# Attention stage of a graph network: ScalarE copies the gathers' block numbers between its two groups of rows

## The chip, the cores and the metric

One core of a Trainium2 chip. The metric is the device time of one execution in microseconds (us); the median of three executions is given. The engines are TensorE (PE; its weight loads are PEld), VectorE (DVE), ScalarE (ACT), GpSimd (POOL) and SyncE (SP), which only issues transfers here.

## What is computed

Four graph layers run over 6250 nodes with 128 features and 106250 edges. The change lies in the fourth, an attention with five anchors:

```
combined = concatenate([x[src], x[dst]], axis=1)
b   = softmax(leaky_relu(combined @ edge_w.T + edge_b, 0.01), axis=1)
ep  = b @ edge_anchor
agg = zeros_like(xp).at[src].add(ep).at[dst].add(ep)
return xp + 0.5 * agg
```

The products of `x` with the two halves of `edge_w` are five numbers for each node. They are made once (P for the source side, Q for the destination side). For each edge the kernel then looks P up by its source and Q by its destination, adds them, makes the softmax, and adds the five weights to the source node and to the destination node.

## The kernel before, in words

The edges lie in 832 tiles of 128. One iteration of the attention loop takes 16 tiles (four groups of four), so there are 52 iterations; the loops' bodies hold two iterations, `u` = 0 and 1, because most buffers are doubled. The engines work it as one pipeline, each with its own hand-written order, and meet at semaphores:

- POOL (lines 854 to 862) fetches P for 12 of the 16 tiles: it waits for `idx16` (the block numbers of that iteration have been copied) and for `logits_done` (the buffer `p_rows[u]` was read two iterations before), then it issues 12 indirect DMAs, line 767. They read `p_table` and count on the semaphore `gathered[u]`.
- ACT (lines 1252 to 1262), in iteration `it`: `rows_ahead(it + 1, 1 - u, g)` for g = 0 and 1, then the exponentials `y5` (line 1258), then `stage_16(it + 2, u)` (line 1173), which copies the 16 block numbers of iteration it + 2 into `stage16[u]` for POOL, then `copy_sources` (line 1196), then `rows_ahead` for g = 2 and 3. `rows_ahead` makes the one-hot rows of the destinations (lines 939 to 945) and, for g = 0 and 1, those of the sources (lines 1183 and 1191). Ahead of line 1183 it waits on `scattered` until TensorE's by_source products of the same group of the iteration before have read the buffer.
- PE (lines 1708 to 1735), in iteration `it`: waits for `logits_done`; looks Q up for the first group of it + 1 (line 1661); turns the source rows (1686); looks P up for four tiles (1694); then four times: look-up of another group (1661) and `by_source` (1667, fp32); at the end 32 small `by_destination` products (1672).
- DVE (lines 2712 to 2782), in iteration `it`: waits for `gathered[u]` and for `q_looked` (the four look-ups of line 1661); sums the logits (2755); adds the fetched rows (2757, which counts `logits_done`); leaky relu, maximum, subtraction (2761 to 2763, `soft_in`); columns (2729); after the exponentials the softmax's sum, reciprocal and products (2768 to 2770), the parts, the matrices for by_source (2749), and `take_sources` (2703 to 2707).
- SP loads the destinations of a group, 256 KB, each time that ACT has read the former ones at line 940.

The lines that set the order around the change are these.

```
act.wait_ge(soft_in, it + 2)
nc.scalar.activation(y5, z5, ACT.Exp).then_inc(soft_exp, 1)
stage_16(it + 2, u)
copy_sources(it + 1)
```

```
pool.wait_ge(idx16, it + 1)
pool.wait_ge(logits_done, it + 1)
for t in range(LOOKED, L16):
    gather(p_rows[u][:, t, :], p_table, stage16[u][:, t:t + 1], gathered[u])
```

`idx16` is counted twice ahead of the loop and `logits_done` starts at 2, so POOL's iteration it + 2 needs ACT's copy and DVE's line 2757 of iteration it.

Of the kernel before, what the change touches and what calls it, by code (L numbers as in the profile page):

```python
# [28 lines left out]
LOOKED = 4  # L29
# [4 lines left out]
ITERS = GROUPS // 4  # L34
# [39 lines left out]
def gnn_stack(nc, x, src, dst, edge_type, Wl1, bl1, Wr1, gamma0, beta0, Wl2, bl2, Wr2,  # L74
# [3 lines left out]
    with ctx:  # L78
# [3 lines left out]
        def sem(name):  # L82
            return ctx.enter_context(nc.semaphore(name))
# [176 lines left out]
        L16 = 4 * GT  # L260
# [122 lines left out]
        gathered = [sem(f"gathered{g}") for g in range(4)]  # L383
# [29 lines left out]
        logits_done = sem("logits_done")  # L413
# [453 lines left out]
        def _(act):  # L867
# [65 lines left out]
            def one_hot_rows(it, g, to, used, used_at, meanwhile=None):  # L933

                k = it * 4 + g
                act.wait_ge(dst_in[g % 2], 16 * (it * 2 + g // 2 + 1))

                act.wait_ge(used, used_at)
                nc.scalar.activation(to[0], dst_b[g % 2][:, :], ACT.Abs, bias=neg_row[0][:, bass.ds(k, 1)])
                nc.scalar.activation(to[1], dst_b[g % 2][:, :], ACT.Abs, bias=neg_row[1][:, bass.ds(k, 1)]).then_inc(oht_abs, 1)  # L940
                if meanwhile:
                    meanwhile()
                act.wait_ge(oht_abs, k + 3)
                nc.scalar.activation(to[0], to[0], ACT.Relu, bias=1.0, scale=-1.0)
                nc.scalar.activation(to[1], to[1], ACT.Relu, bias=1.0, scale=-1.0).then_inc(oht_ready, 1)
# [221 lines left out]
            relu_hidden()  # L1167
            sqrt(sd[:, :], var[:, :], 2 * DENSE + 5 + CHUNKS_IN_PASS)

            def stage_16(it, u):  # L1170

                act.wait_ge(logits_done, it + 1)
                nc.scalar.activation(stage16[u][:, :], p_row_i[:, bass.ds(it * L16, L16)], ACT.Copy).then_inc(idx16, 1)  # L1173

            def rows_ahead(it, u, g):

                lo = lo_l3[u][:, g * GT:(g + 1) * GT, :]

                def source_distances():

                    act.wait_ge(scattered, 4 if isinstance(it, int) else it * 4 + g - 3)
                    for j in range(GT):
                        last = nc.scalar.activation(lo[:, j, :], iota[:, 0:P], ACT.Abs,
                                                    bias=neg_lo[:, bass.ds(it * L16 + g * GT + j, 1)])
                    last.then_inc(lo_abs, 1)

                one_hot_rows(it, g, [oht_l3[:, g, h, :] for h in range(2)], q_looked, it * 4 + g + 1,
                             source_distances if g < 2 else None)
                if g < 2:
                    act.wait_ge(lo_abs, it * 2 + g + 1)  # L1190
                    nc.scalar.activation(lo, lo, ACT.Relu, bias=1.0, scale=-1.0).then_inc(lo_ready, 1)

            def copy_sources(it):

                act.wait_ge(src_turned, it + 1)
                nc.scalar.activation(src_rows, bank[6][:, 0:LOOKED * P], ACT.Copy).then_inc(src_copied, 1)
# [48 lines left out]
            copy_projected(steps_of(PROJ) - 1)  # L1245
            act.wait_ge(zeros_done, 1)
            stage_16(0, 0)
            stage_16(1, 1)
            copy_sources(0)
            act.wait_ge(soft_in, 1)  # L1250
            nc.scalar.activation(n5[0], n5[0], ACT.Exp).then_inc(soft_exp, 1)
            with act.Fori(0, ITERS // 2) as i2:
                for u in range(2):
                    it = i2 * 2 + u
                    for g in range(2):
                        rows_ahead(it + 1, 1 - u, g)
                    act.wait_ge(soft_in, it + 2)
                    nc.scalar.activation(y5, z5, ACT.Exp).then_inc(soft_exp, 1)
                    stage_16(it + 2, u)
                    copy_sources(it + 1)  # L1260
                    for g in range(2, 4):
                        rows_ahead(it + 1, 1 - u, g)
# [1571 lines left out]
```

## Time and profile before

| | us |
|---|---|
| median of 3 executions | 5300.39 (5296.77 to 5312.35) |
| the profiled execution | 5294.73 |
| its span, first to last instruction | 5292.9 |
| PE busy | 3378.9 (64%) |
| DVE busy | 2400.0 (45%) |
| POOL busy | 2265.7 (43%) |
| ACT busy | 1369.7 (26%) |

The attention loop lies in the last quarter of the span, from about 4100 to 5270 us. A row of the timeline is one or several instructions of one line in order of time; the bracket behind it gives the idle time of the engine and what ended it. "remote" stands where the profile could not tell what ended it, and "issue" where the engine waited for nothing that the profile shows.

### The profile page before, as it was taken

How to read it: one execution, taken by the hardware profiler on the slowest of the kernel's cores; microseconds unless marked ns; L12 is line 12 of the kernel's file. 1: busy time of each engine (PE TensorE's matmuls, PEld its weight loads, DVE VectorE, ACT ScalarE, POOL GpSimd, SP SyncE). 2: the span in 40 equal slices, each digit the busy share in tenths (PEclk: the TensorE clock that was granted, in tenths of full speed). 3: DMA queues.
4: the chain of work that ended last, by engine and by line, in shares of the span. 5: the costliest groups of instructions: out<-in, count | busy, mean ns of one | idle time of the engine just before them, and what ended most of it. 6: DMA issues, size and time to landing. Idle time of an engine off the chain costs nothing.

```text
span 5292.9 us, 65458 instructions
## 1 busy us (share of the span) xinstructions
PE 3378.9 (64%) x18669; PEld 2194.1 (41%) x18670; DVE 2400.0 (45%) x6266; ACT 1369.7 (26%) x3030; POOL 2265.7 (43%) x2364
## 2 busy tenths in 40 slices
PE   2699996998734334333333376676696577777776
PEld 2254453444422222222223343333344455555555
DVE  5866666334612222222222222222247566666666
ACT  2655551000400000000000000000002566666665
POOL 3000001000066666666656666666621555555552
PEclk7799998999856666666655577777797666777767
DMA  2211113221712222222221122323230222222222
GB/s 76 59 75 76 50 74 125 84 87 73 202 47 64 68 70 64 69 68 65 69 62 45 46 82 80 90 81 84 79 93 23 45 50 51 50 50 50 50 51 60
DMA packets 265797, 368.93 MB, mean 70 GB/s; under 512 B 64035, under 2 KB 194634, under 8 KB 260666
## 3 DMA queue, kind: packets, MB, share of 16 engines
q1 hardware_dynamic: 187830, 248.24, 14.7%
q0 software_dynamic: 74464, 114.31, 10.2%
q10 hardware_dynamic: 3364, 4.69, 0.3%
q8 instruction: 68, 1.11, 0.1%
q14 instruction: 71, 0.58, 0.0%
HBM read 261.10 MB, written 105.93 MB: 69 GB/s over the span
## 4 chain that ended last, share of the span: by engine, by line
PE 33%; issue 19%; another core or an unknown queue 16%; DVE 14%; POOL 12%; DVEq 3%; DMA 2%; ACT 1%; ACTq 1%; POOLq 0%; SPq 0%
PE psum L1478 14%; POOL GS L767 12%; PE psum L1391 4%; PE psum L1410 4%; PE psum L1348 3%; DVE GS L2074 2%; DMA GS<-xw_table,stage 1%; DVE O L2749 1%; DVEq L2074 1%; PE psum L1543 1%; PE psum L1369 1%; DVE HT L2729 1%; PE psum L1594 1%; PE psum L1595 1%
## 5 line engine op out<-in xcount | busy, mean ns | idle before, releaser
L767 POOL DMA_INDIRECT GS<-xw_table,stage x1664 | 1576.4, 947 | 1440.7 <-issue 1073.0
L1410 PE MATMUL psum<-GS 128*128 128x96 f32 x3328 | 607.8, 343 | 601.5 <-DMA GS<-xw_table,stage 462.3
L1478 PE MATMUL psum<-HA,HT 128*128 128x512 fp8e4 (+1 forms) x3822 | 852.2, 370 | 38.8 <-DVE HT L2258 38.8
L767 POOL DMA_INDIRECT HA<-p_table,stage x624 | 600.5, 962 | 579.4 <-ACT stage L1173 354.2
L1410 PEld LDWEIGHTS psum<-GS 128*128 128x128 f32 x3328 | 566.5, 254 | 650.6 <-issue 638.6
L2088 DVE TENSOR_TENSOR HA<-HA,psum 128x96 f32 x208 | 52.9, 255 | 1584.9 <-remote 1143.2
L2074 DVE TENSOR_SCALAR GS<-iota,HT,wt 128x96 f32<-128x96 f32 x1680 | 453.1, 354 | 213.5 <-issue 212.2
L1478 PEld LDWEIGHTS psum<-HA,HT 128*128 128x128 bf16 x3822 | 360.0, 99 | 370.9 <-DVE HT L2258 39.4
L1369 PE MATMUL psum<-Wcat,codes 128*128 128x512 f32 x196 | 177.8, 1062 | 459.9 <-DVE codes L2567 395.5
L1127 ACT ACTIVATE HA<-psum 128x392 fp8e4<-128x392 f32 x784 | 349.7, 495 | 261.8 <-PE psum L1348 238.7
L876 ACT ACTIVATE stage<-edge_cols 128x16 int32<-128x16 int32 (+1 forms) x104 | 22.1, 215 | 1315.0 <-remote 853.0
L1391 PE MATMUL psum<-Wcat,HT 128*128 128x512 fp8e4 (+1 forms) x1080 | 303.2, 430 | 66.9 <-issue 51.1
L1667 PE MATMUL psum<-O,HA 128*128 128x245 f32 x832 | 252.1, 461 | 40.0 <-issue 20.8
L1369 PEld LDWEIGHTS psum<-Wcat,codes 128*128 128x128 f32 x196 | 56.7, 319 | 519.0 <-issue 519.0
L1667 PE MATMUL psum<-O 128*128 128x245 f32 x832 | 246.3, 451 | 38.3 <-issue 20.3
L1348 PE MATMUL psum<-edge_cols 128*128 128x196 bf16 x1568 | 239.1, 260 | 48.3 <-ACT HA L1127 28.9
L882 ACT ACTIVATE HT<-psum 128x512 f32<-128x512 f32 x49 | 29.3, 597 | 846.7 <-PE psum L1370 608.0
L2749 DVE TENSOR_TENSOR O<-HA,psum 128x980 f32<-128x980 f32 x208 | 242.8, 1167 | 0.0
L1667 PEld LDWEIGHTS psum<-O,HA 128*128 128x128 f32 x832 | 191.0, 239 | 76.7 <-issue 41.3
L1667 PEld LDWEIGHTS psum<-O 128*128 128x128 f32 x832 | 185.7, 233 | 71.3 <-DVE O L2749 25.7
L1391 PEld LDWEIGHTS psum<-Wcat,HT 128*128 128x128 bf16 x1080 | 118.2, 113 | 221.9 <-issue 153.9
L1348 PEld LDWEIGHTS psum<-edge_cols 128*128 128x128 bf16 x1568 | 117.5, 99 | 214.5 <-ACT HA L1127 92.0
(414 smaller groups left out, 4687.6 us busy)
## 6 DMA issues: line engine op xcount, KB each, us to landing
HT<-dst_rows SPq DMA_DIRECT2D x212, 256.0 KB
xw_table<-HT SPq DMA_DIRECT2D x100, 512.0 KB, 3.2
adj<-HA SPq DMA_DIRECT2D x13, 3136.0 KB, 9.1
GS<-xw_table,stage POOLq DMA_INDIRECT x1664
Wcat<-adj SPq DMA_DIRECT2D x45, 512.0 KB
HA<-adj SPq DMA_DIRECT2D x13, 1600.0 KB
HA<-adj SPq DMA_DIRECT2D x13, 1536.0 KB
HA<-adj SPq DMA_DIRECT2D x20, 512.0 KB
```

The source lines that it names most:

```text
L767: nc.gpsimd.indirect_dma_start(out=to, out_offset=None, in_=table, in_offset=bass.IndirectOffsetOnAxis(ap=idx, axis=0)).then_inc(done, 16)
L1127: nc.scalar.activation(placed_at[s][:, :, i * 8:i * 8 + 8].rearrange("p b (w d) -> p b w d", d=NODES_IN_TILE), bank[6 + i % 2][:, 0:2 * KE ...
L1348: last = nc.tensor.matmul(bank[6 + h][:, j % 2 * KEYS:(j % 2 + 1) * KEYS], by_lo[k % 4][:, j, :], by_key[k % 4][:, j, :], start=True, stop ...
L1369: nc.tensor.matmul(bank[2 + c][:, :], own, Wcat[1][:, c * 4 * P:(c + 1) * 4 * P], start=True, stop=True)
L1391: last = nc.tensor.matmul(bank[2 + n % 4][:, 0:w], Hs4[:, CHUNK * c + i, t, :], chunk_tile[place_of(n)][:, i * GW:i * GW + w], start=(i == ...
L1410: last = nc.tensor.matmul(bank[h][:, 0:WINDOW], G3[g][:, j, :], S_pair[h][:, t, :], start=(t == 0), stop=(t == 2 * GT - 1))
L1478: last = nc.tensor.matmul(bank[s][:, 0:w], Hs4[:, b, t, :], adj_tile[s][:, b * GW:b * GW + w], start=(b == 0 and t == 0), stop=(b == SRCS ...
L1543: nc.tensor.matmul(bank[s][:, 0:w], Hs4[:, FINAL + i, t, :], chunk_tile[place_of(n)][:, i * GW:i * GW + w], start=(i == 0 and t == 0), sto ...
L1594: nc.tensor.matmul(bank[2 + 2 * s][:, :], tT[s][:, 0:P], Wcat[0][:, 0:4 * P], start=True, stop=True)
L1667: return nc.tensor.matmul(bank[2][:, 0:245], lo_l3[u][:, t, :], M_l3[:, t, :], start=False, stop=False, skip_group_check=True)
L2074: last = V.tensor_scalar(S_pair[s][:, j, :], iota[:, 0:WINDOW], dl_pair[:, bass.ds(k * 2 * GT + j, 1)], wt[:, bass.ds(k * 2 * GT + j, 1)], ...
L2749: V.tensor_tensor(M_l3[:, at, :].rearrange("p j (d a) -> p j d a", a=A5), hi_l3[:, at, :].unsqueeze(3).broadcast_to([P, GT, 49, A5]), b5[: ...
```

## The change

`stage_16(it + 2, u)` moves ahead of the exponentials, between `rows_ahead` of group 0 and `rows_ahead` of group 1. In place of its wait for `logits_done` it waits inside the loop for `gathered[u]`: that the gathers of iteration it, which read the same `stage16[u]`, have landed. The two copies ahead of the loop wait for nothing now. Nothing else is changed: POOL still waits for `idx16` and `logits_done`, and the order of DVE, PE and SP stays.

```diff
-            def stage_16(it, u):
-
-                act.wait_ge(logits_done, it + 1)
+            def stage_16(it, u, rounds=None):
+
+                if rounds is not None:
+                    act.wait_ge(gathered[u], 64 * 2 * ITERS + 16 * (L16 - LOOKED) * rounds)
                 nc.scalar.activation(stage16[u][:, :], p_row_i[:, bass.ds(it * L16, L16)], ACT.Copy).then_inc(idx16, 1)
...
                     it = i2 * 2 + u
-                    for g in range(2):
-                        rows_ahead(it + 1, 1 - u, g)
+                    rows_ahead(it + 1, 1 - u, 0)
+                    stage_16(it + 2, u, i2 + 1)
+                    rows_ahead(it + 1, 1 - u, 1)
                     act.wait_ge(soft_in, it + 2)
                     nc.scalar.activation(y5, z5, ACT.Exp).then_inc(soft_exp, 1)
-                    stage_16(it + 2, u)
                     copy_sources(it + 1)
```

## Rows read from the trace of the kernel before

**Rows 1.** The page: span; costliest groups (busy, mean ns | idle before, releaser).

```profile
span 5292.9 us, 65458 instructions
...
L767 POOL DMA_INDIRECT HA<-p_table,stage x624 | 600.5, 962 | 579.4 <-ACT stage L1173 354.2
```

**Rows 2.** Waits, 4200 to 5200 us: us in total, times, longest us.

```profile
DVE HA L2755 <- remote: 350.9, 46, 7.7
POOL HA L767 <- ACT stage L1173: 325.8, 46, 7.2
...
PE psum L1672 <- issue: 153.1, 142, 2.0
```

**Rows 3.** Timeline of one iteration, DVE, ACT and POOL: start, us, instruction.

```profile
4598.18 0.41 DVE L2755 TENSOR_REDUCE HA<-psum 128x80 f32<-128x240 f32 x1 [7.60 <-remote]
...
4601.97 0.21 ACT L1173 ACTIVATE stage<-edge_cols 128x16 int32 x1
...
4602.98 1.07 POOL L767 DMA_INDIRECT HA<-p_table,stage  x1 [7.06 <-ACT stage L1173]
...
4612.44 0.61 ACT L1191 ACTIVATE O<-O 128x512 f32<-128x512 f32 x1
...
4616.93 0.94 POOL L767 DMA_INDIRECT HA<-p_table,stage  x1 [0.30 <-issue]
...
4620.12 0.41 DVE L2755 TENSOR_REDUCE HA<-psum 128x80 f32<-128x240 f32 x1 [7.60 <-remote]
4620.13 1.28 ACT L1183 ACTIVATE O<-iota,edge_cols 128x128 f32<-128x128 f32 x4 [5.85 <-remote]
...
4621.23 0.23 DVE L2757 TENSOR_TENSOR HA<-HA 128x80 f32<-128x80 f32 x1
...
4624.94 1.06 POOL L767 DMA_INDIRECT HA<-p_table,stage  x1 [7.06 <-ACT stage L1173]
```

**Rows 4.** Timeline of PE in the same iteration.

```profile
4606.43 3.63 PE L1667 MATMUL psum<-O 128*128 128x245 f32 x8 [1.04 <-DVE O L2749]
...
4610.12 1.93 PE L1667 MATMUL psum<-O 128*128 128x245 f32 x8
4611.89 0.35 PE L1661 MATMUL psum<-HA 128*128 x8
4612.09 3.56 PE L1667 MATMUL psum<-O 128*128 128x245 f32 x16
4615.78 0.17 PE L1672 MATMUL psum<-HA,HT 128*128 128x15 bf16 x1
...
4619.99 1.16 PE L1672 MATMUL psum<-HA,HT 128*128 128x15 bf16 x28 [0.54 <-issue]
```

**Rows 5.** Timeline of DVE, the last two iterations.

```profile
5235.36 0.41 DVE L2755 TENSOR_REDUCE HA<-psum 128x80 f32<-128x240 f32 x1 [7.67 <-remote]
...
5250.01 0.41 DVE L2755 TENSOR_REDUCE HA<-psum 128x80 f32<-128x240 f32 x1 [0.30 <-PE psum L1661]
```

**Rows 6.** Windows: stretch, us, busy (x instructions) of PE, PEld, DVE, ACT, POOL; PEclk.

```profile
4200.00:5200.00 1000.00, 718.31 (x5104) 561.99 (x5104) 647.84 (x1556) 630.11 (x1322) 522.59 (x544) 0.70 0.25 50
...
4602.98:4615.70 12.72, 11.64 (x60) 9.13 (x59) 9.44 (x18) 9.82 (x19) 9.67 (x11) 0.72 0.34 69
4615.70:4619.95 4.25, 0.68 (x4) 0.45 (x4) 0.00 (x0) 0.00 (x0) 1.87 (x2) 1.00 0.36 53
...
4619.95:4622.28 2.33, 1.91 (x38) 1.78 (x38) 2.16 (x11) 2.15 (x6) 0.00 (x0) 0.60 0.00 0
4622.28:4624.93 2.65, 1.42 (x14) 0.86 (x13) 2.62 (x7) 1.88 (x6) 0.00 (x0) 0.50 0.00 0
```

**Rows 7.** Windows of other runs of gathers: start of the attention loop, second hop.

```profile
4163.16:4172.20 9.04, 7.95 (x69) 6.24 (x68) 8.94 (x18) 6.68 (x11) 7.01 (x7) 1.00 0.32 66
4172.20:4180.30 8.10, 3.08 (x8) 1.72 (x8) 0.68 (x1) 4.06 (x9) 4.71 (x5) 0.78 0.20 38
...
3113.54:3127.50 13.96, 13.63 (x67) 8.17 (x65) 5.37 (x20) 0.00 (x0) 10.61 (x12) 0.82 0.32 86
3127.50:3135.90 8.40, 3.97 (x10) 1.13 (x11) 0.00 (x0) 0.00 (x0) 4.53 (x5) 0.78 0.38 109
```

## The prediction

> **What bounds the kernel now.** I read the page first, for the gathers of `p_table`: 624 of them, 962 ns each, and 354.2 us of POOL's idle time end with ACT's copy of the block numbers, line 1173 [rows 1]. That is the wait that the edit goes at. Then the list of waits over 1000 us of the attention loop, for who waits longest: DVE stands 350.9 us at the first operation of its iteration, line 2755, 46 times, 7.6 us each [rows 2]. Then the timeline of one iteration, for the order of events. It repeats from iteration to iteration: line 2755 starts at 4598.18 and at 4620.12, so the period is 21.94 us; there are 48 such periods between the start of the loop and its last iteration.
>
> Counted from line 2755 at 4598.18, POOL's first gather starts at 4.80, right after the copy at 3.79; the twelfth ends at 4617.87, that is 19.69; and the next line 2755 starts 2.25 after that [rows 3]. So the period reads as 4.80 until the gathers start, 14.89 of gathers and 2.25 behind them. The last iteration has no gathers beside it, and its period is 14.65 (5235.36 to 5250.01) [rows 5]. The gathers cost 7.3 us an iteration.
>
> How they cost it decides this case. DVE does not wait there for the gathers in flight: they are those of the iteration after, as ACT has copied their block numbers only in this iteration. Left is `q_looked`. The look-up that it needs last was in PE's array at 4611.89 [rows 4], and DVE went on at 4620.12. ACT's line 1183 was released in the same moment, 4620.13 [rows 3]; it waits for the by_source products that ended at 4612.05 [rows 4]. And PE itself slowed down: after 4615.78 its small products came one in 1.4 or 0.7 us, until 4619.99, when 28 went through in 1.16 us [rows 4]. So three engines are held until about 2.1 us after POOL's last gather. What holds them is PE's side: its products are done but not reported.
>
> The windows show how PE comes to be held. I count matmuls and weight loads together and call them PE instructions. The loop has (5104 + 5104)/45.5 = 224 of them an iteration [rows 6]. From the first gather on, PE did 119 at full pace in 12.72 us, then 8 in 4.25 us [rows 6]. At the start of the loop, with another spacing, it was 137 in 9.04 us, then 16 in 8.10; in the second hop 132 in 13.96 us, then 21 in 8.40 [rows 7]. Three stretches of gathers with the same picture: PE gets through 119 to 137 instructions, then crawls at about 2 a microsecond until the gathers are over. I read this as an allowance in instructions: during the 17.0 us of a hold (14.89 + 2.1) it is 119 + 8 = 127 here, 153 at the start of the loop, and about 132 + 3.1 x 2.5 = 140 in the hop. The other 100 or so of an iteration must be done in the gap between a release and the next first gather. That gap is 4.98 us now and holds 76 + 27 = 103 of them [rows 6].
>
> The Trainium skill, "NOTIFIC — the notification-queue block", section 7.1, says that the block which writes out the instruction records holds its producers back when its internal queues are full rather than lose a record, and that its stall counter would show an engine throttled that way. That is a rule that speaks against this change, since it, too, would make the hold a matter of PE's instruction count; no run here shows that this block is the cause, and by it the sum would be that of the forecast below.
>
> **The change, part by part.**
>
> The copy itself: 0.21 us on ACT [rows 3], moved, not added. It now stands behind line 1191 of group 0, which starts at 4612.44 and ends at 4613.05, so at about 14.9 of the iteration before. It delays group 1 of the rows by 0.2 us at most; behind it on ACT stand lines 939 and 940 of group 1 and, through line 940, one of SP's four loads. ACT idles 5.85 us right behind these [rows 3], so this costs nothing as long as ACT is held there. The look-up copy behind the exponentials comes 0.1 us earlier, which is worth nothing.
>
> The new wait, for the gathers of iteration it: they ended before the line 2755 of iteration it - 1, some 15 us before ACT comes to it. Cost 0 now. If they were late, the six ACT operations of group 1, the exponentials and so DVE's softmax would stand behind it; I see nothing that would make them so late.
>
> What it brings: POOL no longer waits for the copy, only for line 2757, which ends at 4621.46. From the copy's end (4602.18) to the first gather it took 0.80 [rows 3]; the same from 4621.46 gives 4622.26, 2.14 us into the iteration in place of 4.80. So each run of gathers starts up to 2.66 us earlier. I take 2.65.
>
> What is late next: the gap. If the gathers start 2.65 us earlier, the gap is 4.98 - 2.65 = 2.33 us. In its first 2.33 us PE did 76 instructions; the other 27, those of 4622.28 to 4624.93, move under the gathers [rows 6]. Until the small products begin, PE now needs 119 + 27 = 146 in the hold; it has 127 to 153, and the row nearest to this loop's steady state says 127. With 127, 19 are left over, that is 9 or 10 by_source matmuls. They run after the release at 0.24 to 0.45 us each (1.93 and 3.63 us for 8) [rows 4], 2.2 to 4.5 us, and the 64 cheap instructions of line 1672 (1.2 us) come behind them instead of in the gap. So the next hold starts with some 60 more to do, PE does not reach the look-ups before it, and DVE has to wait for them after the release. The lag does not heal: the gathers start 2.14 us after line 2755 however late PE is.
>
> **The sum.** In the state that this runs into, a period is: hold 17.0, then PE's work from where it was held to the last look-up, then 2.1 to the next gather. PE instructions: 224 less 140 in the hold (middle of 127 and 153) less some 16 in the last 2.1 us (by_source at 0.24 to 0.45 us for two) leaves 68. That is two groups of by_source, two groups of look-ups (64 instructions) and a little: 2 x 1.93 + 2 x 0.35 = 4.6 us at the high clock, 2 x 3.63 + 0.7 = 8.0 at the low one. I take 5.7, near the high one, since PE idles more and the granted clock was 1.00 in the crawl [rows 6]. Period 17.0 + 5.7 + 2.1 = 24.8, 2.85 more than now; times 48 is 137 us. Against the profiled execution, 5294.7, that is 5431.7; I say 5430. The median of the three runs is 5.7 us above the profiled one, less than my uncertainty, and I leave it out. With 153 in the hold 55 remain, about 4.1 us, period 23.2, +1.3, 5356; with 127 and the low clock 9 us or more, 28.1, 5590. This case's own range is 5355 to 5590.
>
> **Rivals.**
>
> 1. The hold ends with the gathers whatever PE has to do. Then the period is 2.14 + 14.89 + 2.25 = 19.3; 2.65 x 48 = 127 us less, 5168. For it: DVE's wait of 7.6 us is 7.7 at its longest in 46 iterations [rows 2], so the release does follow the gathers closely as long as PE's look-ups are through, and 153, as at the start of the loop, would be enough for 146 [rows 7]. Against: in the steady state the crawl begins at 119 [rows 6].
>
> 2. The gathers start early only in part. Group 0's by_source is reported at about PE instruction 82 of a hold instead of 55; if that report is held, ACT's copy comes 3 us after the release, POOL starts at 3.8, the period is 20.9 in such iterations: 5294.7 - 48 x 1.0 = 5245. Alternating with case 1 it is 5206.
>
> 3. No gain: the gap settles near 4.9 us again by one delay or another, or the new wait keeps the copy as late as it was: 5295.
>
> The deciding point between rival 1 and the forecast is whether PE can do 146 instructions in a hold.
>
> **Chances.** Forecast, slower: 0.57. Rival 1: 0.15. Rival 2: 0.18. Rival 3: 0.10. The prediction is 5430. The range of 8 in 10 leaves out rival 1 (0.15) and the top of the slow case (0.05): 5200 to 5520. About 0.3% is what a measurement of this kernel can tell from no change; faster by more than that 0.33, within it 0.10, slower 0.57.
>
> **What would show it.** In the profile after: the list of waits no longer has POOL waiting for ACT's copy in either case. First step: first gather 2.1 to 2.2 us after line 2755. Second step: in a hold PE crawls while by_source, line 1667, is not yet finished (before, only line 1672 crawled), and by_source matmuls follow line 2755. Third step: line 2755 comes 4 us or more after the release instead of 0.1, ended by PE's look-up, line 1661, and the period is 23 us or more. If line 2755 keeps coming 2.25 us after the last gather with a period of 19.3, the reading of the hold as an allowance is wrong. If POOL waits for ACT's copy again, it is rival 2.

## The result, and the profile after

The changed kernel took 5508.91 us in the median of four executions (5471.09 to 5531.02), the kernel before beside it 5303.64. The ratio is 1.0378, with a 95% interval of 1.0319 to 1.0438: slower, by 205 us. The profiled execution took 5528.67 us with a span of 5526.9. That it is slower was forecast, and that PE's work would lie behind the gathers and make DVE wait; what keeps PE back is another thing than the one forecast, as the traces below show. The forecast of 5430 is 79 us short of the median, which lies 11 us inside the upper end of the range, 5520. A later run showed something that the prediction had no row for: on another chip of the same kind the same change costs nothing (change_again, below).

All but some 10 us of the loss arises between the first and the last iteration of the attention loop, so the loop is to be read. Its iterations again start at the reduction of the logits, which is now line 2756. These are three of its rows in the timeline of DVE: the first of a steady iteration, one in the middle, and the last iteration.

```profile
4166.26 0.40 DVE L2756 TENSOR_REDUCE HA<-psum 128x80 f32<-128x240 f32 x1
...
4716.49 0.41 DVE L2756 TENSOR_REDUCE HA<-psum 128x80 f32<-128x240 f32 x1 [2.36 <-PE psum L1662]
...
5468.23 0.40 DVE L2756 TENSOR_REDUCE HA<-psum 128x80 f32<-128x240 f32 x1
```

From the first to the last row are 49 periods: 1301.97 / 49 = 26.57 us on average, where it was 21.94 for the one of [rows 3]. Most are 27.4 long, and eight of the 49 lie between 21.9 and 22.7. Note what ended the idle time: PE's look-up of the logits, line 1662, 2.36 us. In [rows 3] this wait was 7.60 us and "remote".

The list of waits over the same 1000 us as [rows 2] names what is new (who waited for whom, us in total, times, longest):

```profile
ACT HT L1197 <- remote: 471.9, 38, 14.8
...
PE psum L1695 <- ACT HT L1197: 315.5, 29, 13.3
POOL HA L767 <- ACT stage L1174: 281.3, 23, 12.8
DVE HT L2730 <- remote: 246.8, 106, 4.2
POOL HA L767 <- DVE HA L2758: 127.8, 14, 12.7
```

In what follows a report is the semaphore count by which PE tells another engine that a product is done; the hold is the time from the first gather of an iteration until the reports are through again, and its end, some 2 us behind the last gather, is the release.

ACT stands 12.4 us each time in front of its copy of the turned source rows, line 1197, and PE stands behind it in front of the look-up of P, line 1695. DVE's long wait at the reduction is gone; instead it waits at line 2730 (the columns), which needs PE's by_destination products. The timeline of PE, in the iteration that starts at 4716.49, shows the order (start, us, instruction, idle before and what ended it):

```profile
4716.31 3.56 PE L1668 MATMUL psum<-O 128*128 128x245 f32 x16
4719.71 1.20 PE L1673 MATMUL psum<-HA,HT 128*128 128x15 bf16 x32
4720.98 0.46 PE L1662 MATMUL psum<-HA 128*128 x8
4721.30 0.64 PE L1687 MATMUL psum<-ident,O 128*128 128x128 f32 x3
4722.26 0.31 PE L1687 MATMUL psum<-ident,O 128*128 128x128 f32 x1 [0.32 <-issue]
4722.98 0.23 PE L1662 MATMUL psum<-HA 128*128 x3 [0.40 <-issue]
4724.40 0.25 PE L1662 MATMUL psum<-HA 128*128 x3 [1.20 <-issue]
4725.13 0.17 PE L1662 MATMUL psum<-HA 128*128 x1 [0.47 <-issue]
4736.54 2.68 PE L1695 MATMUL psum<-HT 128*128 128x250 bf16 x12 [10.52 <-ACT HT L1197]
4739.02 2.75 PE L1668 MATMUL psum<-O,HA 128*128 128x245 f32 x8
...
4718.77:4722.60 3.83, 3.41 (x50) 2.62 (x48) 2.14 (x5) 3.30 (x9) 2.92 (x4) 1.00 0.35 71
4718.77:4726.10 7.33, 4.25 (x58) 3.12 (x56) 2.83 (x6) 3.30 (x9) 5.65 (x6) 0.84 0.23 39
```

The last two rows are windows from the first gather on, with the columns of [rows 6]: PE instructions, as the prediction counts them, are 50 + 48 by the time that the rows are turned, and 58 + 56 when PE stops. And ACT and POOL in the same iteration, then DVE's columns:

```profile
4717.76 0.20 ACT L1174 ACTIVATE stage<-edge_cols 128x16 int32 x1
...
4721.82 0.25 ACT L1260 ACTIVATE HA<-HA 128x80 f32<-128x80 f32 x1
4735.89 0.60 ACT L1197 ACTIVATE HT<-psum 128x512 bf16<-128x512 f32 x1 [13.82 <-remote]
...
4718.77 0.94 POOL L767 DMA_INDIRECT HA<-p_table,stage  x1 [12.10 <-ACT stage L1174]
...
4733.32 0.94 POOL L767 DMA_INDIRECT HA<-p_table,stage  x1 [0.30 <-issue]
...
4723.14 0.69 DVE L2730 TENSOR_TENSOR HT<-rows,wt 128x1024 bf16<-128x1024 bf16 x1 [2.20 <-remote]
4727.39 0.69 DVE L2730 TENSOR_TENSOR HT<-rows,wt 128x1024 bf16<-128x1024 bf16 x1 [3.55 <-remote]
...
4730.26 0.69 DVE L2730 TENSOR_TENSOR HT<-rows,wt 128x1024 bf16<-128x1024 bf16 x1 [2.04 <-remote]
```

PE had turned the rows, line 1687, by 4722.57. ACT was free from 4722.07 and got the report at 4735.89, 1.63 us after the last gather had ended. So for 13.3 us the work was done and not reported. The by_destination products ahead of it (line 1673) were all done by 4720.91, and DVE, which needs one group of them for each of its columns, went on with the second at 4723.14, the third at 4727.39 and the fourth at 4730.26, all while gathers still ran. So a late report needn't wait for the release: they come in PE's order, some 3 to 6 us apart here, and the one for the turned rows is far back in the row. In the kernel before, ACT's same copy waited for PE only three times in 53, and that 3.2 us in all. The period reads 2.28 until the first gather, 17.12 from there to the release at 4735.89, and 8.05 of PE's work behind it (copy, look-up of P, two groups of by_source, two of logits): 27.45. In the eight short iterations the same report came 8.7 to 10.8 us behind the first gather, as in the one that starts at 4611.04, with its first gather at 4613.64:

```profile
4624.42 0.60 ACT L1197 ACTIVATE HT<-psum 128x512 bf16<-128x512 f32 x1 [7.48 <-remote]
```

### The profile page after: what moved, and what is told of

It reads as the page before. It is cut to its first block, busy times and chain, and to the rows that moved or that the text cites. A ratio compares the mean times of both kernels' runs of the same rounds, so it can differ in the third digit from the quotient of the medians.

```text
span 5526.9 us, 65405 instructions
## 1 busy us (share of the span) xinstructions
PE 3275.2 (59%) x18669; PEld 2137.6 (39%) x18670; DVE 2421.6 (44%) x6266; ACT 1359.5 (25%) x3030; POOL 2288.8 (41%) x2364
## 3 DMA queue, kind: packets, MB, share of 16 engines
q1 hardware_dynamic: 187830, 248.24, 14.2%
## 4 chain that ended last, share of the span: by engine, by line
PE 35%; another core or an unknown queue 24%; issue 15%; POOL 10%; ACT 7%; DVE 6%; DVEq 2%; ACTq 1%; DMA 1%; POOLq 0%; SPq 0%
PE psum L1479 14%; POOL GS L767 10%; PE psum L1392 3%; PE psum L1349 3%; PE psum L1411 3%; PE psum L1668 3%; PE psum L1695 2%; PE psum L1544 1%; DMA GS<-xw_table,stage 1%; DVE GS L2075 1%; ACT HA L940 1%; DVEq L2075 1%; ACT HA L939 1%; ACT O L1184 1%
## 5 line engine op out<-in xcount | busy, mean ns | idle before, releaser
L767 POOL DMA_INDIRECT HA<-p_table,stage x624 | 622.7, 998 | 772.6 <-ACT stage L1174 353.7
L1695 PE MATMUL psum<-HT 128*128 128x250 bf16 x636 | 139.7, 407 | 492.9 <-ACT HT L1197 426.3
L2730 DVE TENSOR_TENSOR HT<-rows,wt 128x1024 bf16<-128x1024 bf16 x208 | 143.6, 692 | 347.5 <-remote 328.6
L1695 PEld LDWEIGHTS psum<-HT 128*128 128x128 bf16 x636 | 85.5, 142 | 537.3 <-ACT HT L1197 438.6
L1668 PE MATMUL psum<-O,HA 128*128 128x245 f32 x832 | 218.1, 414 | 13.4 <-issue 12.3
L1668 PE MATMUL psum<-O 128*128 128x245 f32 x832 | 219.9, 416 | 7.4 <-issue 5.3
```

The source lines that it names most:

```text
L767: nc.gpsimd.indirect_dma_start(out=to, out_offset=None, in_=table, in_offset=bass.IndirectOffsetOnAxis(ap=idx, axis=0)).then_inc(done, 16)
L1668: return nc.tensor.matmul(bank[2][:, 0:245], lo_l3[u][:, t, :], M_l3[:, t, :], start=False, stop=False, skip_group_check=True)
L1695: last = nc.tensor.matmul(looked_p[j], src_rows[:, j * P:(j + 1) * P], Pp_part[t], start=(t == 0), stop=(t == PARTS - 1))
L2730: V.tensor_tensor(S_in_fours[:, g, :, :], row_code, dl_b[:, bass.ds(it * L16 + g * GT, GT)].unsqueeze(1).broadcast_to([P, 2 * P, GT]), ALU ...
```

## The experiments

The count theory is the prediction's: PE gets through a limited number of instructions in a hold, and the change asks for more. Beside it stand three others. Order: ACT's new order or its new wait costs the time. Chain: the report of the turned rows falls under the gathers. Report: the general form of it, built on the first four runs: only the first few dozen PE instructions behind the first gather report at once, the others mostly at the release. The kernels ran on several chips. On some the kernel before takes 5303 to 5335 us, on others 4582 to 4589; which it was stands with each run and turned out to matter.

**The start alone.** To the changed kernel one wait of POOL is added:

```diff
                     pool.wait_ge(logits_done, it + 1)
+                    pool.wait_ge(soft_exp, it + 1)
```

> The changed kernel with one wait more: POOL starts its gathers only after the exponentials of the iteration (some 4.9 us after line 2756, as in the kernel before, where it was 4.80). ACT's new order and its new wait stay. Two theories say that the early start alone costs the time: the count theory of the prediction (PE gets through 119 to 153 instructions under the gathers and needs 146) and the chain theory (the report that PE has turned the source rows falls under the gathers, so ACT's copy of them and PE's look-up of P stand until the release). Both expect period 21.9 to 22.1, 5290 to 5320 us, and ACT's line 1197 some 3.9 us after line 2756. The order theory (ACT's copy between its two groups, or the wait on the gathers, costs the time) expects 5450 to 5550, as in the changed kernel.

Measured: 5303.51 us, ratio 0.9998 (0.9989 to 1.0008), before at 5302.83. ACT's order and its wait on the gathers cost nothing when the gathers start late: the order theory falls. The loss comes with the early start of the gathers. The next kernel has the same with soft_in, one step earlier.

> The changed kernel with one wait more: POOL starts after DVE's subtraction of the maxima (line 2764), just ahead of the exponentials, some 4.4 us after line 2756 in place of 2.1 (changed) and 4.8 (before). The chain theory expects that PE's turn is reported by 3.9 us, ahead of the first gather, so that ACT's line 1197 stays at 3.9 us and 0.4 us an iteration is won: period 21.5, 5275 to 5290 us. The count theory expects 107 instructions wanted more in the hold per 0.4 us of 10 a microsecond, that is 123 against 127 to 153: no loss, the same 5275 to 5290, or a first sign of lag, up to 5350. The order theory expects 5450 to 5550.

Measured: 5298.18 us, ratio 0.9994 (0.9984 to 1.0004). No lag, but no gain clear of the noise either, so the expected 13 to 28 us are missing. POOL's rows, in the iteration whose line 2758 starts at 4686.64, show where they are:

```profile
4691.10 1.42 POOL L767 DMA_INDIRECT HA<-p_table,stage  x1 [6.56 <-DVE HA L2766]
4692.82 1.04 POOL L767 DMA_INDIRECT HA<-p_table,stage  x1 [0.30 <-issue]
...
4705.40 0.94 POOL L767 DMA_INDIRECT HA<-p_table,stage  x1 [0.31 <-issue]
```

The first gather takes 1.42 us here and 1.07 in [rows 3]. The last one ends 19.70 us into the iteration, with a start at 4.46, and in [rows 3] at 19.69, with a start at 4.80. The earlier start is lost within the first gather, which takes 0.35 us more; what stretches it was not tried.

**The wait taken from PE.** The look-up of P uses the copy of the iteration before:

```diff
-                pe.wait_ge(src_copied, it + 1)
...
-                        last = nc.tensor.matmul(looked_p[j], src_rows[:, j * P:(j + 1) * P], Pp_part[t],
+                        last = nc.tensor.matmul(looked_p[j], src_rows2[u][:, j * P:(j + 1) * P], Pp_part[t],
```

> The changed kernel, where PE's look-up of P for the first four tiles doesn't wait for ACT's copy of this iteration but uses the copy of the iteration before, in a second buffer; all four look-ups go to one PSUM bank. The number and order of PE's instructions stay at 224 an iteration, and the gathers start early. Left out: the P terms of the first four tiles are not those of their edges. The count theory expects it slow still, since the number of instructions is the same: period 23 or more, 5360 to 5530 us. The chain theory expects that PE no longer stands 10.5 us in front of line 1695: PE goes on to its allowance, and after the release 2.7 us of look-ups and at least one group of by_source (1.9 to 3.6 us) are no longer to be done; period 19.5 to 23, 5180 to 5340 us.

Measured: 5487.34 us, ratio 1.0364 (1.0335 to 1.0392), before at 5302.83. The count theory's range holds it; that of the chain theory doesn't. But the run separates them less than I meant it to. Its waits over 1000 us of the loop are:

```profile
ACT GS L1198 <- remote: 239.1, 20, 14.6
DVE HT L2732 <- remote: 202.2, 95, 5.5
ACT HT L1198 <- remote: 196.2, 17, 15.0
...
4645.31:4662.46 17.15, 9.71 (x75) 6.11 (x74) 8.53 (x19) 3.31 (x10) 12.15 (x12) 0.64 0.15 18
```

I had freed PE, not ACT: its copy still stands 435.3 us in 37 times, with the rows of groups 2 and 3 queued behind it, which PE needs for the logits. That DVE waits for by_destination, too, says that more reports than one are late.

The last row, a window of one of its holds from the first gather to ACT's copy, says more than the time does. PE didn't stop: it did 75 + 74 = 149 instructions, more than the 146 that the prediction wanted. Even so line 2758 came 6.2 us behind the release, at 4668.64, as PE stood 1.87 us at line 1663 for the rows that ACT makes behind its copy, and had a group of by_source and the last logits behind that. So in this kernel PE's count was met and the time was lost all the same, by the report that ACT got late.

**64 instructions fewer.** The changed kernel without the by_destination products:

```diff
-                        for j in range(GT):
-                            last = by_destination(g * GT + j, at[g], S_in_fours[:, g, :, j])
-                        last.then_inc(scattered_d, 1)
+                        pe.sem_inc(scattered_d, 1)
```

> The changed kernel without the 32 by_destination matmuls and their 32 weight loads; PE counts their semaphore itself. Left out: the sums by destination. 160 instructions an iteration are left of 224, 82 of the 146 that had to be done under the gathers. The count theory expects the hold to cost nothing more: period 19.3, 5160 to 5200 us. The chain theory expects that the turned rows are still reported only after the gathers have begun (turn about 4.5 us after line 2756 in the lagging state, gathers from 2.1), so the lagging state stays in most iterations: period 25 to 26.5, 5400 to 5480 us.

Measured: 5282.90 us, ratio 0.9960 (0.9946 to 0.9974), before at 5302.83. Both theories miss. The period is 21.6 us (line 2754 at 4600.02 and 4621.66), and the reason is in three groups of rows: PE's windows from the first gather at 4602.12 (the columns are those of [rows 6]), PE's look-up of P, and ACT and DVE where they take PE's results.

```profile
4602.13:4604.40 2.27, 2.27 (x20) 1.79 (x18) 2.24 (x7) 2.27 (x7) 1.97 (x2) 0.89 0.22 75
4602.13:4607.10 4.97, 4.17 (x39) 3.17 (x37) 4.87 (x14) 4.91 (x12) 4.05 (x4) 0.95 0.19 55
...
4605.58 1.47 PE L1695 MATMUL psum<-HT 128*128 128x250 bf16 x12 [0.75 <-issue]
...
4604.93 0.60 ACT L1197 ACTIVATE HT<-psum 128x512 bf16<-128x512 f32 x1
...
4619.30 0.67 DVE L2702 TENSOR_TENSOR HT<-psum,HT 128x490 f32<-128x490 f32 x1 [7.30 <-remote]
```

The turned rows were done by the 38th PE instruction of the hold (20 + 18), and ACT took them at once. The look-up of P was done by the 76th, at 4607.05, and DVE got it 12.25 us later, at the release. Behind that lie DVE's lines 2702 to 2706, 2.4 us, and they are on the path. With the gathers from 2.10: 2.10 + 15.1 + 2.1 + 2.4 = 21.7. So within one hold an early report passes and a later one doesn't. From this I formed the report theory, though the rows of the changed kernel, with reports that trickle in while gathers run, don't fit its "only".

**One report moved, in the kernel before.** It is the direct test; the number of PE instructions stays, and the gathers start as before:

```diff
-                        if g == 0:
+                        if g == 1:
                             look_up_sources(it + 1)
```

> The kernel before with one thing moved: PE's look-up of P stands behind by_source of group 0 and the logits of group 2 (place g == 1) instead of ahead of them, so it ends about 50 to 58 instructions after the first gather instead of 18; the gathers start at 4.8 us as before. The report theory expects its report to be held until the release in most iterations; DVE then does lines 2702 to 2707 (2.4 us) behind the release: period 24.2, 5380 to 5415 us. The count theory expects no change, since PE does the same number of instructions: 5295 to 5310 us.

The chip was one where the kernel before takes 4582.15 us: 4656.10, ratio 1.0162 (1.0145 to 1.0179). Here DVE's wait at line 2703 is ended by PE's matmul itself each time, 117.4 us in 53, so the report isn't late: it is the look-up that is. A repeat came to such a chip, too:

> The kernel before with PE's look-up of P moved behind by_source of group 0, as in late_p_look_up (on a chip without the hold it came to 1.0162 of before, as DVE waited up to 2.7 us for the look-up). On a chip with the hold the report theory expects the look-up to be the 50th to 58th instruction after the first gather, reported only at the release, 2.4 us of DVE's work behind the release: period 24.2, 5380 to 5415 us. The count theory expects 5295 to 5310 us. On a chip without it: 1.016 again.

4658.88 against 4589.08, ratio 1.0151 (1.0134 to 1.0168). The third came to one where the kernel before takes 5335.05:

> The kernel before with PE's look-up of P moved behind by_source of group 0, once more (on a chip without the hold it was 1.016 and 1.015 of before). On a chip with the hold (before near 5300) the report theory expects: the look-up is the 50th to 58th PE instruction after the first gather in place of the 18th, PE's instructions stay at 224, and the look-up's report comes at the release; DVE waits some 7 us at line 2703 and does its 2.4 us of lines 2703 to 2707 behind the release; period 24.2, 5380 to 5415 us. The count theory expects 5295 to 5310 us, as PE has no more to do than before. On a chip without the hold: 1.015 again.

Measured: 5448.47 us, ratio 1.0215 (1.0198 to 1.0233), that is 113 us or 2.3 an iteration. The count theory expected no change. PE, its windows and DVE of one iteration:

```profile
4708.45 2.19 PE L1694 MATMUL psum<-HT 128*128 128x250 bf16 x12
...
4701.10:4710.70 9.60, 5.96 (x31) 4.69 (x31) 7.33 (x15) 8.40 (x17) 7.25 (x8) 0.54 0.37 85
...
4718.46 0.67 DVE L2703 TENSOR_TENSOR HT<-psum,HT 128x490 f32<-128x490 f32 x1 [9.97 <-remote]
...
4720.83 0.40 DVE L2755 TENSOR_REDUCE HA<-psum 128x80 f32<-128x240 f32 x1
...
4745.18 0.40 DVE L2755 TENSOR_REDUCE HA<-psum 128x80 f32<-128x240 f32 x1
```

The look-up was done at 4710.64, as about the 62nd instruction (31 + 31) behind the first gather at 4701.31, and DVE, which had stood there since 4708.49, got it at 4718.46. Reported at once, it would have held DVE 2.2 us, far ahead of the release. Then its three lines, then line 2755: the period is 24.35, for 24.2 expected. The expected 5380 to 5415 us were reckoned from a kernel before of 5303, as 77 to 112 us more; it was 113 more. The same edit costs 70 to 74 us on the chips without a hold, too, where the iteration is some 7 us shorter and DVE comes to the look-up before it is done; that is another wait.

**The chain moved ahead, with an early start.** The turn stands ahead of by_destination, ACT's copy ahead of its group 1, the look-up of P first in the iteration:

```diff
+                    copy_sources(it + 1)
                     rows_ahead(it + 1, 1 - u, 1)
...
+                    look_up_sources(it + 1)
                     pe.wait_ge(logits_done, it + 2)
...
+                    pe.wait_ge(p_taken, it + 2)
+                    turn_sources(it + 2, u)
                     pe.wait_ge(parts5, it + 2)
```

> The changed kernel (gathers from 2.1 us) with the chain of the turned rows moved: PE turns the source rows of the next iteration right behind the last by_source group, ahead of the by_destination products; ACT copies them ahead of group 1 of the rows; PE looks up P first thing in the iteration. Number of PE instructions unchanged, 224. The report theory, formed on the runs so far, says: of the PE instructions that run after the first gather only about the first 35 to 45 report their end at once, the later ones mostly at the release 2.1 us after the last gather; in the changed kernel the turn (about the 94th) is held. It expects the look-up of P to be among the first 35 here, no wait of 10 us at line 1197, DVE released with the gathers: period 19.3 to 21.0, 5170 to 5260 us. The count theory of the prediction (146 instructions wanted under the gathers, 119 to 153 to be had) expects no cure: 5360 to 5530 us.

> The same moved chain, with POOL held back until DVE's line 2765 just ahead of the exponentials, first gather at 4.45 us. Report theory and count theory both expect the period to be set by the gathers: 21.7 to 21.9, 5285 to 5305 us. A time over 5320 would say that the moved chain itself costs something (the turn ahead of by_destination, or ACT's copy ahead of group 1), to be taken off the result of turn_ahead.

Both came to the chip without a hold: 4677.67 us, ratio 1.0208 (1.0191 to 1.0225), and 4677.32, ratio 1.0209 (1.0192 to 1.0226). The start of the gathers makes no difference there; the moved chain itself costs 2%, some 95 us. Their numbers say nothing on the hold, so the first was run again:

> The kernel of turn_ahead (gathers from 2.1 us, PE's turn ahead of by_destination, ACT's copy ahead of group 1, PE's look-up of P first in the iteration), once more, since its first run came to a chip whose traces show no hold (there 1.021 of before, DVE waiting for its turned rows at 17.1 us a period). If the chip holds PE's reports (before near 5300), the report theory expects the look-up of P among the first 35 PE instructions after the first gather, so that DVE is released with the gathers: period 19.3 to 21.5, 5170 to 5280 us. The count theory expects 5360 to 5530 us. The turn itself stands about 120 instructions into the hold, so its report comes at the release in either case; where ACT's copy, now ahead of its group 1, is what PE then waits for, the period could be 22 to 24. If the chip doesn't hold them: 1.021 again.

With the kernel before at 5303.38 it took 5615.75 us, ratio 1.0593 (1.0575 to 1.0611). Both theories expected less, the report theory by 335 us or more. Why, PE's windows from the first gather at 4706.16 and DVE's rows tell:

```profile
4706.15:4707.90 1.75, 1.75 (x29) 1.63 (x28) 1.72 (x7) 0.44 (x1) 1.44 (x2) 1.00 0.04 1
4706.15:4708.50 2.35, 2.31 (x41) 2.10 (x39) 2.31 (x7) 1.04 (x2) 1.97 (x2) 1.00 0.04 2
4706.15:4710.20 4.05, 3.79 (x54) 3.28 (x52) 2.31 (x7) 2.74 (x7) 3.13 (x4) 1.00 0.04 2
...
4711.98 0.69 DVE L2732 TENSOR_TENSOR HT<-rows,wt 128x1024 bf16<-128x1024 bf16 x1 [3.48 <-remote]
4723.30 0.69 DVE L2732 TENSOR_TENSOR HT<-rows,wt 128x1024 bf16<-128x1024 bf16 x1 [10.62 <-remote]
```

I had misplaced the look-up of P: with the 64 instructions of by_destination ahead of it and PE still behind at the first gather, it is not among the first 35 but done by the 106th (54 + 52). And by_destination itself, done by the 80th, is now under the gathers: DVE's columns wait 10.62 us for it, in the middle of the softmax, so by_block and with it PE's by_source start only behind the release. The mechanism is the same; the move put one more report where it is held. What part of the 312 us is the cost of the moved chain itself was not taken apart.

**Half the gathers.**

> The changed kernel with six gathers an iteration in place of twelve. Left out: the P rows of six of the sixteen tiles are not fetched. Gathers run from 2.1 to 9.6 us after line 2756, release at 11.7. The report theory expects the turned rows still to be reported only at the release, and line 2756 some 8 us after that: period 19 to 20, 5150 to 5200 us. The count theory expects PE never to reach its allowance, as 119 instructions take it longer than the gathers do: period 14.7 to 16, 4940 to 5010 us.

It came to the chip without a hold: 4529.33 us, ratio 0.9886 (0.9869 to 0.9902), before at 4582.15. An iteration takes 14.2 us there (line 2756 at 4111.7 and 4125.9), so six gathers are hidden altogether. How the hold scales with the number of gathers is left open.

**The change itself, again.**

> The changed kernel, unchanged, beside a run of the kernel before on the same chip. On the chip of the last four runs the kernel before took 4582 us in place of 5303, and in their traces PE was never held under gathers. Report theory, if the chip is one that holds PE's reports (before near 5300): 5470 to 5530 us, as first measured. If it is one that doesn't (before near 4580): the early start costs nothing and there is no hold to get rid of; the copy no longer has to be waited for, period 14.9 to 15.3 against some 15.1: 4560 to 4590 us, within 0.5% of before. A rival, that the early gathers collide with something else (SP's loads, DVE) whatever the reports do, expects 1 to 4% slower on either chip.

Measured beside a kernel before of 4589.08 us: 4588.45, ratio 0.9998 (0.9988 to 1.0008). Two of its rows of DVE, and ACT's line 1197 over the whole run (duration, first and last start):

```profile
4204.53 0.41 DVE L2756 TENSOR_REDUCE HA<-psum 128x80 f32<-128x240 f32 x1 [1.39 <-DMA HA<-p_table,stage]
...
4219.51 0.41 DVE L2756 TENSOR_REDUCE HA<-psum 128x80 f32<-128x240 f32 x1 [0.53 <-DMA HA<-p_table,stage]
...
L1197 ACT ACTIVATE HT<-psum x53: 570/577/598, 3738.8 to 4545.9; 128x512 bf16<-128x512 f32 x53
its engine sat idle before it (us, times) until:
  PE psum L1687: 9.1, 16
```

The period is 14.98 us here and 15.3 on average over the loop, POOL's gathers run back to back, and DVE waits a little for their data: 12 x (0.94 + 0.30) = 14.9 is the bound. ACT's copy waits for PE 9.1 us in all, where it was 617.5 us in 49 times in the first trace of the same kernel. So on this chip gathers run through the whole iteration, beside SP's loads and DVE's work, and cost little beyond their own time; the rival with the collision expected 1 to 4% and doesn't hold there. No trace of the kernel before was kept from such a chip, so how early its gathers start is not known.

## Why the prediction was right, and where it was off

**First gather at 2.1 to 2.2: right.** It is 2.10 to 2.84 us, 2.28 in the iteration shown. In this iteration the copy, not line 2758, was last: ACT's group 0 was late, as PE was. POOL still has waits for ACT's copy in its list, which the prediction took as a sign of rival 2; here they come from PE's lag, and the period is longer, not shorter.

**A hold until about 2 us behind the last gather: right.** 17.12 us from first gather to release against 17.0.

**Why PE falls behind: right that it does, wrong in what decides.** The step that failed is "PE now needs 146 in the hold; it has 127 to 153". PE never came to use that allowance: it stopped after 114 (58 + 56) because the look-up of P needs a report from PE to ACT and one back, and the first came at the release. In early_old_sources, where PE didn't have to wait for it, PE got to 149, so 127 wasn't the limit, and the kernel was slow all the same (5487.34). The prediction read the crawl of PE as the hold's only price for PE and counted instructions. [Rows 3] and [rows 4] already had the other half: three engines held by products that were done and not reported. Which reports still pass was the thing to ask. Taken together the traces say that those done by the 38th instruction (early_no_dst) passed, and that those done by the 62nd (late_p_third) and the 76th (early_no_dst) came only with the release; in the kernel before the look-up of P was done by the 22nd, and its early place was what kept 21.94. The change moved the turn to about the 98th. And the changed kernel's own rows show that a late report can come before the release: by_destination 4723.14, 4727.39 and 4730.26, the turned rows in eight iterations 8.7 to 10.8 us behind the first gather. They fit a queue of reports that empties slowly while gathers run better than a fixed line; that is a reading, no run tests it.

Of the second sign, by_source behind line 2756 came (4716.31, 3.56 us), but PE's slow pace fell on lines 1662 and 1687, not on by_source, and began after 98 instructions, where the prediction had 119 to 137.

**Line 2756 late, ended by PE's line 1662: right; its size was the mis-sized term.** The forecast had 5.7 us of PE's work behind the release, for 68 instructions. It was 8.05 us, for 88: two groups of by_source and two of logits, as forecast (4.7 us of the 5.7), but the copy and the look-up of P, 0.65 + 2.68 us, came on top. The period was then 27.45 in place of 24.8 in most iterations. In eight the report came earlier, as at 4624.42, which is 10.8 us behind the first gather in place of 17.1, and the period was 22.34; that pulled the mean to 26.57. The prediction knew nothing of these, and they are why the median lies within its range: 27.45 throughout would be some 43 us more, by these rows above 5520. That part is luck. Against the sum: 26.57 less 24.8 is 1.77, times 49 is 87 us; the start of the loop adds 8.8; 5431.7 + 87 + 9 = 5527, and the profiled execution took 5528.67.

**Rivals.** The hold ended with the gathers for DVE and ACT but left PE with work, so rival 1 (19.3) didn't come about on the chips that hold. Rival 2 had a held report as its mechanism, which is the kind of thing that happened, but of another product (by_source of group 0) and with a start at 3.8 us and a shorter period, which didn't come. Rival 3, no gain and no loss, is what the chips without a hold show, for a reason that it didn't name: there is no hold.

The Trainium skill, "NOTIFIC — the notification-queue block", section 7.1, was given as a rule that speaks against the change, by which a block of records holds producers back. The traces show PE slowed and reports late; no run reads that block's stall counter, so that it is the cause stays open. Every execution on record has a span and a clock from the recording, so whether the reports are late without it is open as well. Open, too, is why some chips hold and others don't, and whether there is a fixed number between the 38th and the 62nd instruction at all. In the kernel before, by_source of group 0 was done by the 55th and ACT went on with it at once, as its row and PE's window say:

```profile
4602.98:4610.10 7.12, 6.08 (x28) 4.33 (x27) 7.05 (x16) 5.76 (x10) 5.59 (x6) 0.50 0.42 77
...
4610.22 1.28 ACT L1183 ACTIVATE O<-iota,edge_cols 128x128 f32<-128x128 f32 x4 [1.24 <-PE psum L1667]
```

In turn_ahead_again, where the same number went through in 1.75 us in place of 7.12, the second group of by_destination was done by the 57th and DVE got it at 4711.98, 4 us late. So the pace seems to count as well as the number, as it would in a queue that empties slowly; no run here takes that apart.

## What to carry to other kernels

Before starting gathers earlier, list the reports between engines that are given during them, in order, and ask which of them another engine is waiting for; the place of a chain from PE to ACT and back just ahead of the gathers was worth more here than the 2.65 us that the earlier start could bring. Where a profile shows engines released together behind the end of a run of gathers, with the work for it long done, count reports and not only instructions. And run such a change on more than one chip: this one was 1.038 on one and 1.000 on another.

## What the runs showed of the hardware that I had not expected

The same kernel before takes 5303 to 5335 us on some chips of this kind and 4582 to 4589 on others. Each chip was met in one session only, so that it is the chip, and not something of the session, isn't shown. The slower ones show the hold; in the changed kernel's trace on a faster one ACT's copy waits 9.1 us for PE in the whole run. It isn't only the attention loop: the first copy of turned rows starts at 3738.8 us in change_again and at 4109.9 in the same kernel's first trace, so 371 us of the difference arise before the loop. By other lines of DVE 34 of them are there at the start (line 1875 at 106.4 and 140.8 us), 33 still at line 2562's last (1418.5 and 1451.7), so some 340 arise behind that, in the part that has the gathers of the hops. A stretch with few gathers, from 200 to 1400 us, doesn't differ like that: it has 12297 PE instructions in the changed kernel's first trace and 12347 in change_again. The windows of both:

```profile
200.00:1400.00 1200.00, 1076.31 (x6149) 559.41 (x6148) 711.25 (x1618) 411.52 (x922) 33.25 (x24) 0.95 0.23 87
...
200.00:1400.00 1200.00, 1088.73 (x6173) 568.21 (x6174) 701.44 (x1634) 404.17 (x930) 32.14 (x22) 0.96 0.24 89
```

A gather's own time is not what differs: most take 0.94 us, with 0.30 between two, on both.
